# Gate and up projections by token tile, weights in four column chunks, and an activation that is turned through DRAM, in a fused two-layer adaLN/FFN kernel

## Chip, cores and metric

The kernel runs on one core of a Trainium2 chip, as one program. The metric is the device time of one execution in microseconds. Before the change it is 393.52 us, the median of 3 runs (393.29 to 393.7).

## What is computed

Two residual layers over 1024 tokens (32 batches of 32) with 512 channels. Cut to what matters:

```
# layer 0, condition: gated FFN with a LoRA branch whose matrices are picked per batch
gate = x @ W_gate.T + LoRA(x, A_gate[id], B_gate[id]) * 0.5      # 512 -> 1376, rank 16
up   = x @ W_up.T   + LoRA(x, A_up[id],   B_up[id])   * 0.5
act  = silu(gate) * up
y    = act @ W_down.T + LoRA(act, A_down[id], B_down[id]) * 0.5  # 1376 -> 512
# layer 0, ffn: one effective 512x512 matrix from low-rank parts
x = x + y @ W_eff.T + bias
# layer 1: condition with top-2 experts, then RMS norm and an int8-like quantized gated FFN
c = x @ W.T + 2 * sum_e gate_e * (x @ A_e) @ B_e
q, s = quant(rmsnorm(c));  Wgq, Wuq, Wdq = quant rows of Wg, Wu, Wd   # round to -127..127
h = silu(q @ Wgq.T * s * sg) * (q @ Wuq.T * s * su)
x = x + quant(h) @ Wdq.T * s2 * sd
```

## The kernel before

**Precision.** Layer 0 keeps float32 accuracy by splitting each operand into a rounded high part and the rest: ScalarE writes the high half (`copy`, into a `..._hl[HI]` tile), VectorE the low half (`lo`), and TensorE makes three products (`THREE`: high·high, high·low, low·high). So each weight tile costs one ScalarE and one VectorE pass.

**Tiling.** The 1024 tokens are two halves (`n`) of 512. For each half the 1376 hidden channels are 11 tiles of 128 (`FT`), and a step `s` is one of the 22. `gate_up(s)` forms gate and up for 128 channels (output rows) by 512 tokens (output columns): per projection 12 matmuls of 512 columns and, for LoRA, 6 of 256 (two groups of eight batches). `silu` and `make_act` leave the activation with channels on partitions, as `down(s)` wants it: 12 matmuls of 512 columns and 6 of 256, accumulated in four banks over 11 steps. TensorE's order is written out by hand: `gate_up(s+1)`, `down(s)`, and so on. The weights are double-buffered by step (`wg_raw`, `wg_hl`), loaded by SyncE (SP).

**Layer 1's weights** are quantized while the second half runs. For each of 11 tiles `f`: SP loads `nat` (512 KB) and `wdx` (256 KB); VectorE takes maxima (`wq_max`, L1025 and L1028); ScalarE scales (`wq_scale`, L715); VectorE rounds to bf16 (`wq_round`, into `nq`); SP issues three DMA transposes (`turn`, L380 to L382). `nat` and `nq` have two buffers each, and `load_nat(f)` waits for the rounding of tile `f-2`. In the loop of SP `load_nat(f+1)` stands ahead of `turn(f-1)`:

```
for f in range(2, FT):
    wg_1(f + 3)
    wd_1(f + 2)
    load_wdx(f + 1)
    load_nat(f + 1)
    turn(f - 1)
```

All engines and both DMA queues take their instructions strictly in the written order; waits are on semaphores. After the last `down` come `cond` (layer 1's condition), `lora_down(1)`, `z` (W_eff), and the quantized FFN.

Of the kernel before, what the change touches and what calls it, by code (L numbers as in the profile page):

```python
# [4 lines left out]
P = 128  # L12
T = 1024
H = 512
F = 1376
# [34 lines left out]
STEPS = NH * FT  # L50

VU_SLOT = (0, 1, 1, 0)
VU_TURN = (1, 2, 4, 5)
STEP0_TURN = 3
C_FIRST = 17 + 4 * FT
# [6 lines left out]
def build(nc, a, scratch, out):  # L62
# [26 lines left out]
    x_raw = [sb(f"x_raw{n}", [P, KT, NB], fp32) for n in range(NH)]  # L89

    W0 = top[0]
    ad_raw = sb("ad_raw", [P, BATCH, FT * RANK], fp32)
    wg_raw = sb("wg_raw", [P, 2, 2 * H], fp32)
    wg_hl = sb("wg_hl", [P, 2, 2, 2 * H], f32r)
    wd_raw = sb("wd_raw", [P, 2, H], fp32)
    wd_hl = sb("wd_hl", [P, 2, 2, H], f32r)
    b_raw = sb("b_raw", [P, 2, 2, 2 * P], fp32)
    b_hl = sb("b_hl", [P, 2, 2, 2, 2 * P], f32r)
    W1 = top[0]

# [18 lines left out]
    D1 = top[0]  # L119
    consts = sb("consts", [P, CONSTS], fp32)  # L120
# [25 lines left out]
    wdx = sb("wdx", [P, H], fp32)  # L146
    wsd_b = wdx
# [51 lines left out]
    oh_lang = sb("oh_lang", [P, TILES, E8], fp32)  # L199
# [28 lines left out]

    def hf(t):
        return t.bitcast(fp32)  # L230

    with ExitStack() as ctx:
        def sem(name):
            return ctx.enter_context(nc.semaphore(name))
# [71 lines left out]
        def _(sp):  # L306
# [30 lines left out]
            with sp.Fori(0, AGU_SP) as b:  # L337
                load_a("a_gu", agu, b, agu_sp)
# [1404 lines left out]
```

## Time and profile before

| | |
|---|---|
| median of 3 runs | 393.52 us |
| span of the profiled execution | 391.3 us (its own time outside the profiler isn't recorded; the median lies 2.2 us above the span) |
| TensorE busy | 379.0 us, 97% |
| VectorE, ScalarE, GpSimd busy | 252.1, 184.1, 140.7 us |
| DMA | 59.89 MB, mean 153 GB/s |

Busy time is a union over the span, and a busy TensorE means only that matmuls follow one another without a gap. The spacing from one block's start to the next block's start is what a block costs.

### The profile page before, as it was taken

Reading aid. Unit: us, or ns where it says so; the run is one execution under the profiler, and the core shown is the slowest. Engines: PE = TensorE matmul, PEld = TensorE weight load, DVE = VectorE, ACT = ScalarE, POOL = GpSimd, SP = SyncE. Lnnn points to the kernel's source line nnn. Section 1 sums busy time; section 2 is a strip of 40 time slices with the busy share of each in tenths; the row PEclk is TensorE's granted clock in tenths of the full one; section 3 lists DMA queues with packets and bytes.
Section 4 is the critical chain, followed back from the end, with each engine's and each line's share of the span. In section 5 each row is a group of like instructions: output and inputs, shape, how many; then the busy total and the mean of one; then the engine's idle time right before and its main releaser. Section 6 shows DMA issues by size and latency. Waiting matters only on the chain.

```text
span 391.3 us, 5936 instructions
## 1 busy us (share of the span) xinstructions
PE 379.0 (97%) x1997; PEld 301.0 (77%) x1997; DVE 252.1 (64%) x485; ACT 184.1 (47%) x307; POOL 140.7 (36%) x138
## 2 busy tenths in 40 slices
PE   8999999999999999999999999999999999899992
PEld 4688888888888988888888888888889874344441
DVE  5876844444454446656777666755585888999982
ACT  5544733333333334434444444643555635676670
POOL 2877887777401061200112130000000124557751
PEclk9999999999999999999999999999999999999998
DMA  7878443445423232632999987554658422323412
GB/s 293 278 230 304 161 142 142 157 165 162 140 94 107 82 94 97 238 115 86 308 271 239 218 197 181 134 109 147 210 119 179 173 54 54 39 56 85 119 62 80
DMA packets 53126, 59.89 MB, mean 153 GB/s; under 512 B 34658, under 2 KB 37500, under 8 KB 52976
## 3 DMA queue, kind: packets, MB, share of 16 engines
q1 hardware_dynamic: 48055, 48.20, 43.2%
q0 software_dynamic: 4320, 10.49, 8.5%
q10 hardware_dynamic: 728, 0.93, 0.7%
q8 instruction: 11, 0.18, 0.2%
q14 instruction: 12, 0.09, 0.1%
HBM read 50.02 MB, written 2.11 MB: 133 GB/s over the span
## 4 chain that ended last, share of the span: by engine, by line
PE 85%; DVE 5%; DMA 4%; ACT 2%; issue 1%; SPq 1%; DVEq 0%; ACTq 0%
PE ps L1353 31%; PE ps L1402 15%; PE ps L1359 8%; PE ps L1478 6%; PE ps L1524 5%; PE ps L1382 4%; PE ps L1598 4%; PE ps L1628 3%; DMA wg_raw<-w_gu_dram 2%; PE ps L1496 2%; PE ps L1344 2%; PE ps L1414 1%; PE ps L1326 1%; PE ps L1531 1%; DVE hqs L1261 1%
## 5 line engine op out<-in xcount | busy, mean ns | idle before, releaser
L1353 PE MATMUL ps<-x_hl,wg_hl 128*128 128x512 f32 x528 | 128.0, 391 | 0.2 <-ACT wg_hl L574 0.2
L1353 PEld LDWEIGHTS ps<-x_hl,wg_hl 128*128 128x128 f32 x528 | 97.4, 188 | 21.0 <-DVE wg_hl L930 0.9
L496 POOL DMA_INDIRECT b_raw<-b_gu_dram,idx_all x44 | 44.3, 1006 | 93.6 <-DVE b_hl L930 83.3
L1402 PE MATMUL ps<-act_hl,wd_hl 128*128 128x512 f32 x264 | 64.0, 391 | 0.0
L1402 PEld LDWEIGHTS ps<-act_hl,wd_hl 128*128 128x128 f32 x264 | 48.2, 188 | 9.1
L1021 DVE TENSOR_TENSOR act_raw<-ps,sil 128x512 f32<-128x512 f32 x22 | 15.2, 689 | 54.6 <-issue 38.0
L1359 PEld LDWEIGHTS ps<-tg_hl,b_hl 128*128 128x128 f32 x264 | 37.3, 190 | 3.3
L1359 PE MATMUL ps<-tg_hl,b_hl 128*128 128x256 f32 x264 | 38.4, 282 | 0.0
L930 DVE TENSOR_TENSOR wg_hl<-wg_raw,wg_hl 128x1024 fp32r<-128x1024 f32 x22 | 26.9, 1224 | 13.2 <-ACT wg_hl L574 12.4
L538 POOL TENSOR_TENSOR qs<-qs,half 128x1 f32<-128x1 f32 x8 | 4.4, 550 | 85.2 <-DVE qs L1225 85.2
L574 ACT ACTIVATE act_hl<-act_raw 128x512 fp32r<-128x512 f32 x22 | 13.9, 633 | 42.3 <-DVE act_raw L1021 42.3
L547 POOL TENSOR_TENSOR g_sb<-g_sb,u_sb 128x459 f32<-128x459 f32 (+1 forms) x23 | 26.5, 1161 | 19.5 <-ACT g_sb L847 19.3
L715 ACT ACTIVATE nat<-nat,winv 128x512 f32<-128x512 f32 x22 | 14.7, 716 | 38.1 <-DVE winv L1033 38.1
L483 POOL DMA_INDIRECT agu<-a_gu_dram,idx_a x23 | 27.0, 1176 | 12.7 <-issue 6.7
L483 POOL DMA_INDIRECT ad_raw<-a_d_dram,idx_a x24 | 24.2, 1009 | 7.3 <-issue 7.3
L661 ACT ACTIVATE sil<-ps 128x512 f32<-128x512 f32 x22 | 12.9, 586 | 27.2 <-PE ps L1359 27.2
L1524 PE MATMUL ps<-wc_lo_hi,x_hl 128*128 128x512 f32 x96 | 23.6, 395 | 0.0
L1598 PE MATMUL ps<-wq_g,qt 128*128 128x459 bf16 (+1 forms) x96 | 22.6, 357 | 1.0 <-DVE g_sb L1252 1.0
L574 ACT ACTIVATE wg_hl<-wg_raw 128x1024 fp32r<-128x1024 f32 x22 | 23.0, 1045 | 0.2 <-DMA wg_raw<-w_gu_dram 0.2
L1478 PE MATMUL ps<-y_hl,we_hl 128*128 128x512 f32 x96 | 23.0, 394 | 0.0
L1598 PE MATMUL ps<-wq_u,qt 128*128 128x459 bf16 (+1 forms) x96 | 22.6, 358 | 0.0
L930 DVE TENSOR_TENSOR b_hl<-b_raw,b_hl 128x512 fp32r<-128x512 f32 x22 | 15.1, 687 | 10.9 <-ACT b_hl L574 10.9
(171 smaller groups left out, 585.0 us busy)
## 6 DMA issues: line engine op xcount, KB each, us to landing
wg_raw<-w_gu_dram SPq DMA_DIRECT2D x22, 512.0 KB, 4.0
wd_raw<-w_d_dram SPq DMA_DIRECT2D x22, 256.0 KB, 2.8
nat<-w_nat_dram SPq DMA_DIRECT2D x11, 512.0 KB, 4.8
wdx<-w_nat_dram SPq DMA_DIRECT2D x11, 256.0 KB, 2.6
natd<-wd_nat_dram SPq DMA_DIRECT2D x4, 704.0 KB, 5.0
vu_raw<-w_vu_dram SPq DMA_DIRECT2D x3, 512.0 KB, 9.3
out_dram<-r_sb SPq DMA_DIRECT2D x6, 256.0 KB, 2.0
ws_b<-scale_scratch SPq DMA_DIRECT2D x2, 688.0 KB, 5.5
```

What stands on the lines that cost most here:

```text
L483: gp.indirect_dma_start(out=tile[:, b, :], out_offset=None, in_=a[table].rearrange("e p c -> (e p) c"), in_offset=bass.IndirectOffsetOnAxi ...
L496: gp.indirect_dma_start(out=b_raw[:, slot, g, :], out_offset=None, in_=a["b_gu"], in_offset=bass.IndirectOffsetOnAxis(ap=idx_all[:, f, 2 * ...
L547: nc.gpsimd.tensor_tensor(g_sb[:, slot, cols], g_sb[:, slot, cols], u_sb[:, slot, cols], ALU.mult).then_inc(h_made, 1)
L574: return nc.scalar.activation(o, i, ACT.Copy)
L930: return V.tensor_tensor(o, raw, hf(hi), ALU.subtract)
L1353: mm(bank[:], wg_hl[:, slot, w, gu * H + k * P:gu * H + (k + 1) * P], x_hl[n][:, v, k, :], start=(k == 0 and (w, v) == THREE[0]), stop=False)
L1359: last = mm(bank[:, g * GT:(g + 1) * GT], b_hl[:, slot, w, g, gu * P:(gu + 1) * P], tg_hl[:, n, v, gu, g * GT:(g + 1) * GT], start=False, ...
L1382: last = mm(ps[TD][:, g * GT:(g + 1) * GT], ad_hl[:, slot, w, g * P:(g + 1) * P], act_hl[:, slot, v, g * GT:(g + 1) * GT], start=(first an ...
L1402: last = mm(ps[m][:], wd_hl[:, slot, w, m * P:(m + 1) * P], act_hl[:, slot, v, :], start=(first and (w, v) == THREE[0]), stop=False)
L1478: last = mm(ps[m][:], we_hl[:, w, k, m * P:(m + 1) * P], y_of[n][:, v, k, :], start=(k == 0 and (w, v) == THREE[0]), stop=(k == KT - 1 and ...
L1524: mm(ps[CB[t]][:], x_hl[t // 4][:, w, k, (t % 4) * P:(t % 4 + 1) * P], wc_hl[v][:, k, :], start=(k == 0 and (w, v) == THREE[0]), stop=False)
L1598: last = mm(ps[(G_BANK, U_BANK)[gu][c]][:, 0:CH[c]], qt[:, t, k, :], wq(gu, k, slice(CO[c], CO[c] + CH[c])), start=(k == 0), stop=(k == KT ...
```

## The change

Layer 0's gate and up are formed with tokens on output rows. A step `s` (now 32) is 128 tokens by a chunk of 352 channels (320 in the last chunk): `x_hl` is stationary, the weights `wg_hl` stream. Four steps (`t` = 0 to 3) share a chunk `j`, and there are four chunks per half (8 in all). The weights of a chunk (four pieces of 352 KB) have one buffer, raw and split. LoRA: the 64 rank rows of four batches are doubled to 128, high part in one half of the partitions and low part in the other, so 2 matmuls of 352 columns replace 6 of 256. For that the tokens are permuted (`x_p`), so that a 128-token tile holds batches t, t+4, t+8, t+12.

The activation now has tokens on partitions, and `down` (unchanged, 22 of them, named d) wants channels there: VectorE turns 32x32 blocks (`turn_act`), ScalarE's queue writes a chunk to DRAM in four DMAs (`write_act`), and SP reads it back by tiles of 128 channels (`load_act`). So the `down`s of chunk j-1 run during chunk j, and the last three after all gate and up work. x is loaded a second time unpermuted. `wq_round` moves from VectorE to ScalarE.

```
+CW = (352, 352, 352, 320)
+DONE = ((0, 1), (2, 3, 4), (5, 6, 7), (8, 9, 10))     # the downs that chunk c completes
...
+            def next_nat(f):
+                turn(f - 2)
+                load_nat(f)
+                load_wdx(f)
...
+            for i, d in enumerate(downs_of(NCH + 1)):
+                next_nat(2 + i)
+                load_down(d)
...
+            next_nat(9)
+            sp.wait_ge(gate_ready, STEPS)
             sp.dma_start(wc_raw[:], a["wc_t"]).then_inc(wc_in, 16)
...
+            sp.wait_ge(up_ready, STEPS)
+            sp.dma_start(x1_n[1][:], a["x_t"][:, :, NB:T]).then_inc(x_in[2], 16)
+            next_nat(10)
+            for d in downs_of(NCH + 3):
+                load_down(d)
...
+            def write_act(j):
+                n, c = divmod(j, NCH)
+                nb = CW[c] // 32
+                act.wait_ge(turned, NT * (j + 1))
+                for q in range(4):
+                    act.dma_start(act_t[n, CO0[c]:CO0[c] + CW[c], q * P:(q + 1) * P].rearrange("(b i) m -> i b m", i=32),
+                                  act_s[32 * q:32 * q + 32, 0:nb].rearrange("p b t m -> p b (t m)")).then_inc(act_out, 16)
...
+            for s in range(24, STEPS):                 # ScalarE
+                step(s)
+                wq_scale(s - 23)
+                wq_round(s - 23)
...
+            for s in range(24, STEPS):                 # VectorE
+                step(s)
+                wq_max(s - 22)
...
+            def gate_up(s):
+                pe.wait_ge(silu_done, s)
+                base(s, 0)
+                lora(s, 0)
...
+                    pe.wait_ge(act_made, s - 1)
+                base(s, 1)
+                lora(s, 1)
```

What the change moves, where the prediction rests on it. VectorE in the second half, before: one step of the loop, from the product of gate and up (`act_raw`) to the next step's splits of weights and LoRA rows.

```order
L1021 TENSOR_TENSOR act_raw<-ps,sil 128x512 [waits act_lo,wg_used]
L930 TENSOR_TENSOR ad_hl<-ad_raw,ad_hl 128x256
L930 TENSOR_TENSOR wd_hl<-wd_raw,wd_hl 128x512 [waits wd_hi]
L930 TENSOR_TENSOR act_hl<-act_raw,act_hl 128x512 [waits act_hi]
L1025 TENSOR_REDUCE wm<-nat 128x2
L1028 TENSOR_REDUCE wdm<-wdx 128x4
L1039 TENSOR_SCALAR nq<-nat 128x1024 [waits wq_in0]
L930 TENSOR_TENSOR wg_hl<-wg_raw,wg_hl 128x1024 [waits wg_hi]
L930 TENSOR_TENSOR b_hl<-b_raw,b_hl 128x512 [waits b_hi]
```

The same place now, behind step 24; `b_hl` here is the split of step 26's LoRA rows.

```order
L1112 TENSOR_TENSOR act_raw<-ps,sil 128x352 [waits turned,up_ready,silu_done]
L1120 STREAM_TRANSPOSE act_s<-act_raw 128x11x32 [waits act_out,act_made]
L1125 TENSOR_REDUCE wm<-nat 128x2 [waits nat_in0]
L1128 TENSOR_REDUCE wdm<-wdx 128x4 [waits wdx_in]
L1131 TENSOR_SCALAR ws_f<-wm 128x2 [waits wm_step]
L1133 RECIPROCAL winv<-ws_f 128x2 [waits wm_step]
L1015 TENSOR_TENSOR b_hl<-b_raw,b_hl 64x704 [waits b_hi]
```

The maxima (`wm`, `wdm`) of one layer-1 tile stand between two steps as before, but a step is now 128 tokens by 352 channels; the rounding into `nq` has left the engine, and the 32x32 transposes have come. The next split of LoRA rows stands behind the maxima. SP's queue, before, one pass of the loop in the second half:

```order
L374 DMA wdx<-w_nat_dram 128x512 [waits wdx_used]
L368 DMA nat<-w_nat_dram 128x1024 [waits nat_rounded]
L380 DMA_TRANSPOSE wq_g<-nq 128x4x128 [waits nat_rounded]
L381 DMA_TRANSPOSE wq_u_105<-nq 128x2x128
L382 DMA_TRANSPOSE wq_u_106<-nq 128x2x128
L314 DMA wg_raw<-w_gu_dram 128x1024 [waits wg_lo,wg_hi]
L319 DMA wd_raw<-w_d_dram 128x512 [waits wd_lo,wd_hi]
```

SP's queue now, at the end of the second half (its last tile of layer 1, then the loads of down 19):

```order
L452 DMA wc_raw_117<-wc_t_dram 128x2048 [waits gate_ready]
L454 DMA x_again_115<-x_t_dram 128x4x512 [waits up_ready]
L407 DMA_TRANSPOSE wq_g_112<-nq_109 128x4x128 [waits nat_rounded]
L408 DMA_TRANSPOSE wq_u0_74<-nq_109 128x2x128
L409 DMA_TRANSPOSE wq_u1_113<-nq_109 128x2x128
L396 DMA nat_108<-w_nat_dram 128x1024 [waits nat_rounded]
L401 DMA wdx_110<-w_nat_dram 128x512 [waits wdx_used]
L356 DMA wd_raw_58<-w_d_dram 128x512 [waits wd_lo]
L364 DMA a_f_65<-act_scratch 128x512 [waits act_lo,act_out]
```

The load of `nat` moved from ahead of a tile's three transposes to behind them, and `a_f`, which TensorE needs for down 19, stands behind both. TensorE at the same place, before (the logits `h_logits(0)`, then `down(21)` alone, then `cond(0)`):

```order
L1496 MATMUL ps<-awr,x_raw_51 128x136 [waits awr_in,act_made]
L1496 MATMUL ps<-awr,x_raw_51 128x136 x11
L1382 MATMUL ps<-act_hl,ad_hl 128x256 [waits ad_lo,act_lo,wd_lo]
L1382 MATMUL ps<-act_hl,ad_hl 128x256 x5
L1402 MATMUL ps<-act_hl,wd_hl 128x512 x12
L1524 MATMUL ps<-wc_lo_hi,x_hl_49 128x512 [waits x1_lo,silu_done,wc_lo]
```

and now, the second part of down 18, the logits, and the beginning of down 19:

```order
L1512 MATMUL ps<-act_hl,wd_hl 128x512 x12
L1595 MATMUL ps<-awr,x_raw_51 128x136 [waits awr_in,act_made]
L1595 MATMUL ps<-awr,x_raw_51 128x136 x11
L1492 MATMUL ps<-act_hl,ad_hl 128x256 [waits ad_lo,act_lo,wd_lo]
L1492 MATMUL ps<-act_hl,ad_hl 128x256 x5
```

Three `down`s follow the logits where one did.

## Rows read from the trace of the kernel before

**Rows 1.** The page, parts 1 and 2: busy time and granted clock in 40 slices.

```profile
PE 379.0 (97%) x1997; PEld 301.0 (77%) x1997; DVE 252.1 (64%) x485; ACT 184.1 (47%) x307; POOL 140.7 (36%) x138
...
PEclk9999999999999999999999999999999999999998
```

**Rows 2.** Timeline, TensorE, one step (start, us; then duration of the block).

```profile
54.32 0.88 PE L1359 MATMUL ps<-tg_hl,b_hl 128*128 128x256 f32 x6
55.04 2.91 PE L1353 MATMUL ps<-x_hl,wg_hl 128*128 128x512 f32 x12
...
58.50 0.88 PE L1382 MATMUL ps<-act_hl,ad_hl 128*128 128x256 f32 x6
...
61.96 2.88 PE L1353 MATMUL ps<-x_hl,wg_hl 128*128 128x512 f32 x12
```

**Rows 3.** Busy time by stage of the gate/up/down phase.

```profile
core 0: us, PE busy (x) PEld busy (x) DVE busy (x) ACT busy (x) POOL busy (x), PEclk, DMA share, GB/s
120.00:150.00 30.00, 30.00 (x173) 26.34 (x171) 14.11 (x23) 9.62 (x17) 6.25 (x6) 1.00 0.34 110
...
215.00:245.00 30.00, 30.00 (x159) 25.85 (x158) 18.99 (x31) 14.25 (x24) 6.21 (x6) 1.00 0.82 198
```

**Rows 4.** Timeline of the start: first steps of ScalarE and TensorE.

```profile
9.85 1.06 ACT L574 ACTIVATE x_hl<-x_raw 128x1024 fp32r<-128x1024 f32 x1 [0.70 <-DMA x_raw<-x_t_dram]
...
12.92 0.72 ACT L586 ACTIVATE wg_hl<-vu_raw,consts 128x512 fp32r<-128x512 f32 x1 [0.72 <-DMA vu_raw<-w_vu_dram]
...
30.61 2.99 PE L1353 MATMUL ps<-x_hl,wg_hl 128*128 128x512 f32 x12
```

**Rows 5.** Groups by line and form: one instruction's mean in ns behind the comma.

```profile
L574 ACT ACTIVATE wg_hl<-wg_raw 128x1024 fp32r<-128x1024 f32 x22 | 23.0, 1045 | 0.2 <-DMA wg_raw<-w_gu_dram 0.2
...
L574 ACT ACTIVATE b_hl<-b_raw 128x512 fp32r<-128x512 f32 x22 | 13.7, 620 | 14.4 <-DMA b_raw<-b_gu_dram,idx_all 14.4
...
L930 DVE TENSOR_TENSOR wg_hl<-wg_raw,wg_hl 128x1024 fp32r<-128x1024 f32 x22 | 26.9, 1224 | 13.2 <-ACT wg_hl L574 12.4
...
L930 DVE TENSOR_TENSOR b_hl<-b_raw,b_hl 128x512 fp32r<-128x512 f32 x22 | 15.1, 687 | 10.9 <-ACT b_hl L574 10.9
...
L1025 DVE TENSOR_REDUCE wm<-nat 128x2 f32<-128x1024 f32 x5 | 6.1, 1216 | 3.2 <-DMA nat<-w_nat_dram 3.2
...
L1028 DVE TENSOR_REDUCE wdm<-wdx 128x4 f32<-128x512 f32 x5 | 3.4, 677 | 0.0
...
L715 ACT ACTIVATE nat<-nat,winv 128x512 f32<-128x512 f32 x22 | 14.7, 716 | 38.1 <-DVE winv L1033 38.1
...
L959 DVE COPY ag<-agu 128x512 f32<-128x512 f32 x8 | 2.9, 429 | 0.9 <-DMA agu<-a_gu_dram,idx_a 0.9
```

**Rows 6.** Timeline of SP's queue, one pass (start, time that the issue takes).

```profile
215.74 0.33 SPq L368 DMA_DIRECT2D nat<-w_nat_dram  x1
216.11 1.20 SPq L380 DMA_TRANSPOSE wq_g<-nq  x1
...
218.63 1.25 SPq L382 DMA_TRANSPOSE wq_u<-nq  x1
219.98 0.52 SPq L314 DMA_DIRECT2D wg_raw<-w_gu_dram  x1
```

**Rows 7.** DMA issues: count, KB each, median us from issue to landing.

```profile
wd_raw<-w_d_dram SPq DMA_DIRECT2D x22, 256.0 KB, 2.8
nat<-w_nat_dram SPq DMA_DIRECT2D x11, 512.0 KB, 4.8
...
out_dram<-r_sb SPq DMA_DIRECT2D x6, 256.0 KB, 2.0
```

**Rows 8.** Timeline: a DMA issue on ScalarE's queue, and the end of the phase.

```profile
1.16 0.45 ACTq L578 DMA_DIRECT2D vu_raw<-w_vu_dram  x1
...
265.81 2.94 PE L1496 MATMUL ps<-awr,x_raw 128*128 128x136 f32 x24
268.50 0.96 PE L1382 MATMUL ps<-act_hl,ad_hl 128*128 128x256 f32 x6
```

More of the change, by code:

```diff
@@ L795, in _ @@
             h_copy(0)
+            td_split(1)
             act.wait_ge(wst_ready, 1)
@@ new lines, in _ @@
+            step(20)
+            td_mask(0)
+            step(21)
+            b_split(23)
+            y_out(0)
+            make_act(22)
+            turn_act(22)
+            for q in range(KT):
+                x1_add(q)
+            down_split(downs_of(NCH)[1])
+            wq_max(0)
+            b_split(24)
+            w_split(NCH + 2, 0)
+            make_act(23)
+            turn_act(23)
+            w_split(NCH + 2, 1)
+            for q in range(KT):
+                x1_low(q)
+            wq_max(1)
@@ L1378, in down_lora @@
-            def down_lora(s, slot, first, end):
-                pe.wait_ge(ad_lo, s + 1)
-                for g in range(2):
-                    for w, v in THREE:
-                        last = mm(ps[TD][:, g * GT:(g + 1) * GT], ad_hl[:, slot, w, g * P:(g + 1) * P],
-                                  act_hl[:, slot, v, g * GT:(g + 1) * GT], start=(first and g == 0 and (w, v) == THREE[0]),
-                                  stop=(end and g == 1 and (w, v) == THREE[-1]), skip_group_check=True)
-                return last
@@ L1387, in down @@
[L1387 to L1397 removed]
+                        last = mm(ps[TD][:, g * GT:(g + 1) * GT], ad_hl[0:m, slot, w, g * P:(g + 1) * P],
+                                  act_hl[0:m, slot, v, g * GT:(g + 1) * GT], start=(f == 0 and g == 0 and (w, v) == THREE[0]),
+                                  stop=(f == FT - 1 and g == 1 and (w, v) == THREE[-1]), skip_group_check=True)
@@ L1398, in down @@
+                return last
+            def down(d):
+                n, f = divmod(d, FT)
+                slot, rows = d % 2, rows_of(d)
+                pe.wait_ge(wd_lo, d + 1)
+                pe.wait_ge(act_lo, d + 1)
+                if d == 0:
+                    pe.wait_ge(we_lo, KT)
+                if d == FT:
+                    pe.wait_ge(td_masked, 1)
+                if d:
+                    down_lora(d)
                 for m in range(KT):
-                    if first and n:
+                    if d == FT:
@@ L1400, in down @@
                         pe.wait_ge(x1_made, m + 1)
                     for w, v in THREE:
-                        last = mm(ps[m][:], wd_hl[:, slot, w, m * P:(m + 1) * P], act_hl[:, slot, v, :],
-                                  start=(first and (w, v) == THREE[0]), stop=False)
-                if lora_behind:
-                    last = down_lora(s, slot, first, end)
+                        last = mm(ps[m][:], wd_hl[0:rows, slot, w, m * P:(m + 1) * P], act_hl[0:rows, slot, v, :],
+                                  start=(f == 0 and (w, v) == THREE[0]), stop=False)
@@ L1545, in _ @@
             h_logits(0)
-            down(STEPS - 1, 1, 1, end=True)
+            for d in downs_of(CHUNKS - 1):
+                down(d)
             pe.wait_ge(wc_lo, 1)
```

961 lines of the change are left out of this document (506 added, 455 removed).

## Prediction, made before the changed kernel ran

> **What bounds the kernel now.** I read the page first: TensorE is busy 97% of the span and its clock is granted in full in all but the last slice [rows 1], so below about 390 us the kernel gets only by less work on TensorE, and every gap opened there costs its length. Then the windows: through the whole gate/up/down phase TensorE has 30.00 busy us in 30, while VectorE and ScalarE have 14.1 and 9.6 in the first half and 19.0 and 14.3 in the second, and the DMA share goes from 0.34 to 0.82 in the second half, where layer 1's weights are quantized and turned [rows 3]. The reader is to see slack everywhere but on TensorE, and least of it in the second half. Then TensorE's timeline for what a block costs, by starts: six matmuls of 256 columns take 55.04 - 54.32 = 0.72 us (0.120 each), a `down` (six of 256, twelve of 512, equal to a gate or up block) 61.96 - 58.50 = 3.46 us, hence twelve of 512 take 2.74 us (0.228 each) [rows 2].
>
> **The change on TensorE.** Before, 22 steps of two blocks: 22 x 6.92 = 152.2 us. A 352-column matmul is in no row. From 0.120 at 256 and 0.228 at 512 the line gives 0.161, and 0.147 for 320; the bounds, by columns from either row alone, are 0.157 and 0.165. I take the line, since both ends lie on it. Now a step is 28 matmuls (24 base, 4 LoRA): 24 steps x 28 x 0.161 + 8 x 28 x 0.147 = 141.1 us. The gain is **11.1 us** (bounds 8.5 to 13.5), nearly all from LoRA (264 matmuls of 256 become 128). The 22 `down`s are unchanged.
>
> The Trainium skill (TensorE: Matmul & The Clock Gate, section "Wait — 56ns, not 53.3ns?") gives a warm matmul N/2.4 GHz plus about 2.5 ns, 215.7 ns at 512 columns; by that 352 columns cost 149 ns and the gain would be some 22 us. The trace disagrees, with 228 ns for these float32r operands, and I go by the trace.
>
> **Start.** Step 0's work on TensorE shrinks by 6.92 - 28 x 0.161 = 2.4 us, but what ends it isn't its work. The first chunk's weights are 1408 KB instead of 512 KB, ahead of `vu_raw` 2; a 512 KB piece took about 1.3 to 1.8 us there, so it lands 2.3 to 3.1 us later than the 12.92 us of [rows 4], and ScalarE and VectorE split 2816 columns where they split 1024. So I let step 0 end 0.5 us after the 30.61 of [rows 4]: **+2.9 us** (0 to 5).
>
> **First half.** Chunk weights have one buffer, but between the last gate of a chunk and the first of the next stand an up block (2.25) and a `down` (3.46): 5.7 us to cover one silu (0.45), two ScalarE passes and two VectorE passes of 704 columns. Line from [rows 5]: 0.78 and 0.89 us, 0.68 and 0.80 back to back, about 3.2 us in all. The trip through DRAM: four issues on ScalarE's queue at 0.45 [rows 8], 2.0 us to land as a 256 KB store does, 2.8 as a 256 KB load [rows 7], about 7 us against 13 to 20 us before the `down` is due. Both at nothing; uncovered they'd cost 3 and 7 us per chunk. The 32x32 transposes (32, no row) lie between a copy of 512 columns, 0.43, cut to 352, 0.3, and a tensor-tensor of 512, 0.69 [rows 5]; I take 0.45. On an engine half idle they cost nothing.
>
> Against this change speaks the Trainium skill (DMA: Bandwidth & Descriptors, "Anatomy of one DMA"): each DMA has a fixed cost of about 2.0 us, mostly the write receipt, so a trip through DRAM pays it twice. The trace agrees with its 2.0 and 2.8 us [rows 7]. It changes the sum only where the trip isn't covered, which is the tail below.
>
> **Second half, steps 24 to 31.** Here eight steps carry eight tiles of layer 1's weights; before, a tile had 10.4 us of TensorE beside it, now 4.5 (a step) plus 1.25 `down`s on average, 6.5 us. A tile's circle: rounding on ScalarE releases three transposes on SP (219.98 - 216.11 = 3.9 us of queue), **then** the load of `nat` (4.8 to landing) [rows 6, 7], then the maxima on VectorE (1.22 + 0.68 + 0.3, some 2.1), then scaling (2 x 0.72, 1.25 back to back) and rounding (0.95) on ScalarE [rows 5]. Two buffers allow one circle of some 13 us, with the steps between, per two tiles: TensorE's own pace. Nothing is left for lateness, and what waits in it holds back work that TensorE wants: behind VectorE's wait for `nat` stand the LoRA rows of the step after next and the product of the next one. Walked through, with time 0 where TensorE would begin step 24:
> - Step 23's up ends at -3.5. Behind it ScalarE has 1.4 (weights), 1.25, 1.8 (four issues), four x halves 2.1, rounding 0.95: tile 0 is rounded at 4.0, LoRA rows and silu(24) follow at 5.2, where TensorE wants them at 4.5: **0.7**.
> - SP: 4.0 + 3.9 + 4.8 = 12.7 until `nat` 2 is there, maxima 14.8, the LoRA rows of step 26 (0.8) 15.6. TensorE wants them after step 25 and the gate of 26, at 11.6: **4.0**.
> - At the chunk's end ScalarE's four writes wait for VectorE, which waited for tile 4: down 15 is split about **1.1** late, and tile 4 rounded only at 36.5. `nat` 6: 45.2, maxima 47.3, rows of step 30 48.1; TensorE wants them at 44.3: **3.8**.
> - The same two tiles on: `nat` 8 at 58.0, product and transpose of step 31 at 61.0, four writes 62.8, split of down 18 65.0; TensorE wants it at 61.5: **3.5**.
>
> Sum **+13.1 us** (0 if loads land in 2.8 and VectorE isn't caught; 20 if two more steps are).
>
> **Tail.** Count from the end of step 31's up. TensorE has downs 17 and 18 and the logits (2 x 3.46 + 268.50 - 265.81 = 9.6 us) [rows 2, 8] before down 19. Its operand: product and transpose 1.0, writes 2.8, split of down 18 4.3, scaling and rounding of tile 8 6.4, SP's transposes 10.3, issues of `nat`, `wdx`, `wd_raw`, `a_f` 11.8, landing with 1.3 MB in front 15.8, splits 17. **+7.4**. Behind down 19's split each engine turns to tile 10 (`nat` there at about 15), maxima 19.1, scale and round 21.3, split of down 20 23.3; TensorE wants it at 20.5: **+2.8**. Tail **+10.2 us** (6 to 14). In that is room for the clock: it was granted in full in every slice but the last, in which TensorE runs dry [rows 1]; should it fall from 2.4 to 1.2 GHz in a gap, each `down` run so costs 3.46 us more. Queued behind: `cond(0)` and everything later, unchanged.
>
> **Sum** against the profiled span: 391.3 - 11.1 + 2.9 + 13.1 + 10.2 = 406.4 us. The median of the runs lies 2.2 above the span of before, so 408.6; I say **408**.
>
> **Rivals.** A change under 0.2% (0.8 us) can't be told from none here.
> - *Tail alone* (0.18): layer 1's tiles keep up in steps 24 to 31, for 215 to 245 shows a DMA share of 0.82, not 1, and VectorE a third idle [rows 3]. 391.3 - 11.1 + 2.9 + 10.2 = 393.3, median 395.5. Against it: the loop has no slack by its rows.
> - *Faster* (0.12): `a_f` of down 19 arrives in time, because tile 8 is rounded before the writes matter or SP gets past it early. One mechanism, one place: it decides if the way to `a_f` is under 9.6 us instead of 17. With step loop fine too, 391.3 - 11.1 + 2.9 + 2.2 = 385.3. Against: that order is written in three in-order queues.
> - *Same* (0.04): tail alone with a start that loses nothing, 393 to 394.
> - *DMA is the bound* (0.08): the trip adds some 11 MB to a stage whose share is already 0.82 [rows 3]; writes are 512-byte rows. If steps 20 to 31 ran at the DMA's pace, 1.3 x 80 us, 420 to 430.
> - My forecast (0.58): 399 to 420.
>
> **Numbers.** Likeliest 408. Range 394 to 420, which leaves out faster, same and DMA-bound at their far ends, and takes in the tail alone. Faster 0.12, same 0.04, slower 0.84.
>
> **What would show it.** Blocks of 12 base matmuls at 1.93 us and LoRA pairs at 0.32; TensorE without gaps from step 1 to 23; VectorE waiting on the DMA of `nat` before L1125 in steps 24 to 31 and TensorE waiting on VectorE's `b_hl`; a gap of several us ahead of down 19 that ends with `a_f`, and a smaller one ahead of down 20. Wrong if gaps stand in the first half (the trip or the single weight buffer then isn't covered), if a 352-column matmul costs 0.15 or 0.18, or if `nat` lands before VectorE asks.

## Result, and the profile after

The changed kernel takes **420.07 us** (median of 4 executions, 419.39 to 420.86) against 393.45 us (393.29 to 393.7, 4 executions) on the same chip: ratio 1.067, interval 1.065 to 1.0689. It is 26.6 us slower; the profiled span went from 391.3 to 417.6 us. Here and in the experiments, executions over 1.5% above the fastest of their kernel are left out (417.77 us of nat_first, 410.16 of combined).

The page of the changed kernel, parts 1 and 2, against [rows 1]:

```profile
PE 381.7 (91%) x2098; PEld 318.6 (76%) x2101; DVE 279.0 (67%) x537; ACT 210.3 (50%) x349; POOL 110.0 (26%) x110
...
PE   8899998999999999999869787775899999999994
...
PEclk9889999999999999999998999968999999999999
DMA  8995491856845727340787949897055932122622
```

TensorE, busy 97% before, has holes in two places: the first seven slices (10.4 us each) and slices 20 to 29, that is 198 to 303 us, where layer 1's weights are quantized. The clock falls in both. Between them the middle of the kernel is as tight as it was.

Two blocks in the second half, TensorE's timeline (start, duration):

```profile
226.16 2.08 PE L1460 MATMUL ps<-wg_hl,x_hl 128*128 128x352 f32 x12
228.08 0.32 PE L1469 MATMUL ps<-b_hl,tg_hl 128*128 128x352 f32 x1
228.24 0.32 PE L1471 MATMUL ps<-b_hl,tg_hl 128*128 128x352 f32 x1
228.40 2.08 PE L1460 MATMUL ps<-wg_hl,x_hl 128*128 128x352 f32 x12
```

By starts: 12 base matmuls 1.92 us, the LoRA pair 0.32, a matmul of 352 columns 0.160 us; where blocks of 320 follow each other, a step takes 4.08 us, 0.146 per matmul. The waits of TensorE (total us, times, longest):

```profile
PE ps L1492 <- DVE act_hl L1015: 13.0, 4, 5.6
PE ps L1469 <- DVE b_hl L1015: 6.0, 2, 3.4
PE ps L1460 <- DVE wg_hl L1015: 2.1, 2, 1.9
PE ps L1460 <- ACT sil L739: 2.0, 2, 1.2
PE ps L1512 <- DVE wd_hl L1015: 1.6, 1, 1.6
```

**Where the 26 us are.** Two more rows of the kernel before, the first `cond` and the last sum on VectorE (TensorE's and VectorE's timelines):

```profile
272.05 2.88 PE L1524 MATMUL ps<-wc_lo_hi,x_hl 128*128 128x512 f32 x12
...
384.79 0.36 DVE L1313 TENSOR_TENSOR r_own<-o_own,x1t 128x192 f32<-128x192 f32 x1
```

and the same places after, with the start of step 1 ahead:

```profile
35.24 2.17 PE L1460 MATMUL ps<-wg_hl,x_hl 128*128 128x352 f32 x12
...
301.09 2.91 PE L1623 MATMUL ps<-wc_lo_hi,x_hl 128*128 128x512 f32 x12
...
413.35 0.36 DVE L1416 TENSOR_TENSOR r_own<-o_own,x1t 128x192 f32<-128x192 f32 x1
```

Step 1 starts 4.63 us later, `cond(0)` 29.04 us later, the last sum 28.56 us. The last output is there 4.25 us behind that sum instead of 6.51, which gives 2.3 us back: 26.3 in all. It is 4.2 to 4.3 us in the profile of every changed kernel below; no run shows why. To split the 29.04, each block's spacing by starts is compared with its tight value (1.92, 0.16, 0.72, 2.75 and so on); the excess is what it lost, by an idle wait or by running at half clock.

| part | forecast | measured |
|---|---|---|
| gate and up, work on TensorE | -11.1 | 152.2 - 24 x 28 x 0.160 - 8 x 28 x 0.146 = -12.0 |
| start (with the 2.4 us that step 0's own work shrank by) | +2.9 | 4.63 + 2.4 = +7.0 |
| first half | 0 | +3.6 |
| steps 24 to 31, with down 15 | +9.6 | +14.0 |
| hole ahead of down 18 | +3.5 | +5.7 |
| tail, from down 18 on | +10.2 | +10.6 |
| behind `cond(0)` | 0 | -0.5, and -2.3 for the last landing |

### The profile page after: what moved, and what is told of

It reads as the page before. It is cut to its first block, busy times and chain, and to the rows that moved or that the text cites. A ratio compares the mean times of both kernels' runs of the same rounds, so it can differ in the third digit from the quotient of the medians.

```text
span 417.6 us, 5954 instructions
## 1 busy us (share of the span) xinstructions
PE 381.7 (91%) x2098; PEld 318.6 (76%) x2101; DVE 279.0 (67%) x537; ACT 210.3 (50%) x349; POOL 110.0 (26%) x110
## 4 chain that ended last, share of the span: by engine, by line
PE 55%; DVE 15%; DMA 12%; ACT 7%; SPq 6%; issue 3%; ACTq 2%; POOL 0%; DVEq 0%
PE ps L1460 19%; PE ps L1512 9%; PE ps L1535 5%; PE ps L1623 5%; DMA a_f<-act_scratch 5%; PE ps L1492 2%; DMA wg_raw<-w_gu_dram 2%; DVE hqs L1364 2%; DVE g_sb L1355 2%; DVE u_sb L1358 2%; ACT nat L768 2%; ACTq L691 2%; PE ps L1698 2%; PE ps L1446 2%; DMA act_scratch<-act_s 2%
## 5 line engine op out<-in xcount | busy, mean ns | idle before, releaser
L1460 PE MATMUL ps<-wg_hl,x_hl 128*128 128x352 f32 (+1 forms) x768 | 135.6, 326 | 5.6 <-DVE wg_hl L1015 2.1
L1460 PEld LDWEIGHTS ps<-wg_hl,x_hl 128*128 128x128 f32 x768 | 125.7, 193 | 11.2 <-issue 5.3
L1512 PE MATMUL ps<-act_hl,wd_hl 128*128 128x512 f32 (+1 forms) x264 | 66.9, 404 | 1.6 <-DVE wd_hl L1015 1.6
L1512 PEld LDWEIGHTS ps<-act_hl,wd_hl 128*128 128x128 f32 (+1 forms) x264 | 50.4, 197 | 11.7 <-DVE wd_hl L1015 1.9
L739 ACT ACTIVATE sil<-ps 128x352 f32<-128x352 f32 (+1 forms) x32 | 14.6, 457 | 56.4 <-PE ps L1471 55.2
L1015 DVE TENSOR_TENSOR wg_hl<-wg_raw,wg_hl 128x704 fp32r<-128x704 f32 (+1 forms) x32 | 26.3, 863 | 13.0 <-ACT wg_hl L624 13.0
L1492 PE MATMUL ps<-act_hl,ad_hl 128*128 128x256 f32 (+1 forms) x132 | 21.0, 298 | 13.0 <-DVE act_hl L1015 13.0
L624 ACT ACTIVATE b_hl<-b_raw 64x704 fp32r<-64x704 f32 (+1 forms) x32 | 24.8, 774 | 14.2 <-PE ps L1471 7.4
L1015 DVE TENSOR_TENSOR b_hl<-b_raw,b_hl 64x704 fp32r<-64x704 f32 (+1 forms) x32 | 27.8, 870 | 5.8 <-ACT b_hl L624 4.8
L1469 PE MATMUL ps<-b_hl,tg_hl 128*128 128x352 f32 (+1 forms) x64 | 20.9, 326 | 6.3 <-DVE b_hl L1015 6.0
L624 ACT ACTIVATE wg_hl<-wg_raw 128x704 fp32r<-128x704 f32 (+1 forms) x32 | 23.1, 770 | 4.9 <-PE ps L1471 2.9
L1120 DVE STREAM_TRANSPOSE act_s<-act_raw 128x352 f32<-128x352 f32 (+1 forms) x32 | 17.2, 537 | 11.1 <-DMA act_scratch<-act_s 10.1
```

The lines of the kernel that those rows point to most:

```text
L624: return nc.scalar.activation(o, i, ACT.Copy)
L1015: return V.tensor_tensor(o, raw, hf(hi), ALU.subtract)
L1120: V.transpose(act_s[:, 0:nb, t, :], act_raw[:, 0:CW[c]]).then_inc(turned, 1)
L1460: mm(bank[:, 0:w], x_hl[n][:, v, k, t * P:(t + 1) * P], wg_hl[gu][:, u, k, 0:w], start=(k == 0 and (v, u) == THREE[0]), stop=False)
L1469: mm(bank[:, 0:w], tg_hl[:, HI, gu, t * P:(t + 1) * P], b_hl[:, s % 2, gu * w:(gu + 1) * w], start=False, stop=False)
L1492: last = mm(ps[TD][:, g * GT:(g + 1) * GT], ad_hl[0:m, slot, w, g * P:(g + 1) * P], act_hl[0:m, slot, v, g * GT:(g + 1) * GT], start=(f == ...
```

## Why layer 1's tiles hold up the gates

SP's queue, changed kernel, around the first hole of the second half:

```profile
207.12 1.31 SPq L407 DMA_TRANSPOSE wq_g<-nq  x1
208.48 1.23 SPq L408 DMA_TRANSPOSE wq_u<-nq  x1
209.75 1.25 SPq L409 DMA_TRANSPOSE wq_u<-nq  x1
211.04 0.59 SPq L396 DMA_DIRECT2D nat<-w_nat_dram  x1
```

VectorE:

```profile
210.57 0.55 DVE L1120 STREAM_TRANSPOSE act_s<-act_raw 128x352 f32<-128x352 f32 x1
215.42 1.22 DVE L1125 TENSOR_REDUCE wm<-nat 128x2 f32<-128x1024 f32 x1 [4.30 <-DMA nat<-w_nat_dram]
...
217.54 0.89 DVE L1015 TENSOR_TENSOR b_hl<-b_raw,b_hl 64x704 fp32r<-64x704 f32 x1
```

and TensorE:

```profile
218.48 0.56 PE L1469 MATMUL ps<-b_hl,tg_hl 128*128 128x352 f32 x1 [3.44 <-DVE b_hl L1015]
...
219.13 3.42 PE L1460 MATMUL ps<-wg_hl,x_hl 128*128 128x352 f32 x12
```

Read them downwards. Rounding of tile 0 (ended 207.1) releases three transposes, 3.9 us of issuing; only then goes the load of `nat` 2, which lands 4.4 us later. VectorE stands 4.30 us at `wm`; behind it waits the split of step 26's LoRA rows, and TensorE stands 3.44 us for that. The block behind the hole then takes 3.25 us by starts (219.13 to 222.38) where it should take 1.92. The same wait stands three more times for 3 to 5 us (until 231.6, 251.6 and 265.9); the first held the split of chunk 7's weights (hole of 1.93 us ahead of step 28), the second step 30's rows (2.51), the third step 31's product and with it down 18 (5.57).

## The experiments

Each kernel was timed beside the kernel before on its chip; those of one group below ran on the same chip. A ratio is not exactly the quotient of the two medians. For size: 0.01 is 3.9 us.

| kernel | median us | ratio to before, interval |
|---|---|---|
| changed | 420.07 | 1.067, 1.065 to 1.0689 |
| nat_first | 411.3 | 1.0443, 1.0423 to 1.0464 |
| loads_first | 408.26 | 1.0398, 1.036 to 1.0436 |
| tail_loads | 423.31 | 1.0771, 1.0741 to 1.0801 |
| fill_holes | 419.58 | 1.0675, 1.0623 to 1.0728 |
| third_first | 409.73 | 1.043, 1.0392 to 1.0469 |
| tail_order | 406.22 | 1.0315, 1.0247 to 1.0383 |
| no_trip | 416.83 | 1.0622, 1.0553 to 1.069 |
| gate_whole | 417.31 | 1.0625, 1.0599 to 1.0651 |
| combined | 403.54 | 1.03, 1.0218 to 1.0382 |
| combined_hold | 406.6 | 1.0329, 1.0312 to 1.0346 |
| combined_late | 400.07 | 1.0143, 1.0109 to 1.0178 |
| combined_light | 403.0 | 1.0245, 1.0206 to 1.0285 |

### First group: the order of SP's queue, and the clock

**nat_first**

```
 def next_nat(f):
-    turn(f - 2)
     load_nat(f)
     load_wdx(f)
+    turn(f - 2)
```

> SP issues the loads of nat and wdx of tile f ahead of the three transposes of tile f-2, as before the change; nothing else moves. Theory A (order in SP's queue): nat of tiles 2, 6 and 8 comes 3.9 us earlier, so the 3.44 us gap ahead of step 26's LoRA rows and the 2.51 us gap at step 30 go, and with them the half-clock stretch behind the first (1.3 us); the gap ahead of down 18 loses up to 3 us. Together 7 to 12 us, 408 to 413. Theory B (pace: DMA is full in these steps and a tile's circle is too long in any order): the transposes only come later in turn, gaps move, and the time stays within 2 us of 420.

8.8 us faster, theory A. The order alone, which the change had turned round, was worth a third of the loss: from the start of step 24 to that of down 18 TensorE takes 56.9 us instead of 65.6.

**loads_first**: the load of the next down's operands goes ahead of the transposes too (`load_nat`, `load_wdx`, `load_down(d)`, `turn(f - 2)`).

> As the run before, and the loads of wd_raw and a_f of the next down also stand ahead of the transposes. Theory A: the down operands land 4 us earlier too, which helps where ScalarE waited for a_f (4.8 to 5.5 us each, and queued behind that wait are the scaling and rounding of the next tile): another 2 to 4 us, 405 to 410. Theory B: no more than the run before, within 2 us of 420.

11.8 us faster than the changed kernel, 3.0 of them beyond the run before (their intervals overlap, so this part is not shown). From step 24 to down 18 it takes 53.7 us. The same place of TensorE's timeline, loads_first:

```profile
210.90 2.08 PE L1460 MATMUL ps<-wg_hl,x_hl 128*128 128x352 f32 x12
213.12 0.43 PE L1469 MATMUL ps<-b_hl,tg_hl 128*128 128x352 f32 x1
```

2.22 us from start to start: the hole of 3.44 is down to some 0.3, and the clock is whole behind it. In 200 to 260 us the busy time of TensorE rose from 49.20 to 53.52 us (first row changed kernel, second loads_first; the columns behind PEclk are DMA share and GB/s):

```profile
200.00:260.00 60.00, 49.20 (x278) 45.04 (x277) 40.37 (x71) 36.07 (x58) 4.18 (x4) 0.97 0.81 220
```

```profile
200.00:260.00 60.00, 53.52 (x318) 49.43 (x316) 45.97 (x83) 40.06 (x66) 4.17 (x4) 1.00 1.01 263
```

So the DMA engines, with a share of 0.81, were not the limit in the changed kernel's loop; the same work packed tighter makes it 1.01. Whether they are the limit at 1.01 is another question, which combined_light takes up.

**tail_loads**

```
+for d in downs_of(NCH + 3)[0:2]:
+    load_down(d)
 next_nat(10)
-for d in downs_of(NCH + 3):
-    load_down(d)
+load_down(downs_of(NCH + 3)[2])
```

> Only in the tail: the loads for downs 19 and 20 stand ahead of the transposes of tile 8 and the loads of tile 10. Theory A: a_f of down 19 is issued at about 275.5 instead of 280.9, lands some 4 us earlier behind wc and x, so the 4.22 us gap and the slow clock behind it (1.5 us) go, but nat 10 comes later and the gap ahead of down 20 may grow: net 3 to 6 us, 414 to 417. Theory B (the 2 MB of wc and x in front of it set the landing): 0 to 1.5 us, 418.5 to 420.

Wrong on both sides: 3.2 us slower. SP's queue, tail_loads:

```profile
268.56 0.94 SPq L356 DMA_DIRECT2D wd_raw<-w_d_dram  x1
278.79 0.33 SPq L364 DMA_DIRECT2D a_f<-act_scratch  x1
...
280.11 1.22 SPq L407 DMA_TRANSPOSE wq_g<-nq  x1
```

SP stood 9.3 us at `a_f` until the last chunk's writes had landed, with tile 8's transposes and `nat` 10 behind it, so the hole ahead of down 20 grew from 1.63 to 4.81 us while down 19's stayed at 4.02. Ahead of the transposes `a_f` was issued 2.2 us earlier than in the changed kernel (278.79 against 280.95) and not 5: what held it there was the writes.

**fill_holes**: matmuls with an all-zero stationary operand in the holes (22 of them ahead of down 18, for instance), so that TensorE doesn't idle.

```
+for _ in range(count):
+    mm(bank[:, 0:w], zeros[:], x_hl[1][:, HI, 0, 0:w], start=False, stop=False)
 pe.wait_ge(b_lo, s + 1)
```

> TensorE gets matmuls with an all-zero operand in the holes (5 of 512 columns bf16 in the start, 18 of 352 ahead of step 26's LoRA rows, 22, 16 and 6 of 512 ahead of downs 18, 19 and 20); no operand comes earlier. Theory A (a hole costs its length and then the clock: 2.4 to 1.2 GHz behind the holes at 15, 215, 269 and 284 us): the granted clock stays at 1.00 and 7 to 10 us come back, 410 to 413. Theory B (only the holes' lengths count, or the clock falls for another reason, such as the DMA load): within 1 us of 420, or slower by what the added matmuls overrun.

Theory A's mechanism is there and its price is not. Busy time, granted clock, DMA share and GB/s in the tail, changed kernel:

```profile
274.00:280.00 6.00, 6.00 (x17) 0.50 1.08 371
```

and fill_holes, with the start of its down 19:

```profile
274.00:280.00 6.00, 6.00 (x44) 1.00 1.16 315
...
287.37 1.50 PE L1498 MATMUL ps<-act_hl,ad_hl 128*128 128x256 f32 x6 [3.40 <-DVE wd_hl L1019]
```

Down 18 ran at 2.4 instead of 1.2 GHz, it and the logits behind it ended 3 us earlier, and down 19 still began at 287.4 us, where it had begun at 287.47. Its operand was on its way through DRAM and knows nothing of the clock; what the clock gave back, the next hole took. Ahead of step 28 the same happened: its hole grew from 1.93 to 3.18 us. In a stretch bound by another chain, half clock costs nothing, and a list of excess times counts that loss twice over.

### Second group: the trip, the tail and the start

**third_first** (on loads_first), ScalarE at the end of a chunk:

```
-write_act(j)
 if j and len(downs_of(j - 1)) == 3:
     down_split(downs_of(j - 1)[2])
+write_act(j)
```

> The run with all loads ahead of the transposes (408.3), and on ScalarE the split of a chunk's third down now stands ahead of the four writes of the next chunk's activation. Theory A (down 18 waits for the writes' place in ScalarE's queue, its own operand having landed long before): its split starts some 3.4 us earlier, the 3.97 us gap ahead of down 18 and the half clock behind it (1.1 us) go, but the four writes start 1.5 us later and so does a_f of down 19, whose gap (6.67 us) takes the rest: net 0 to 3 us, 405 to 408. Theory B (down 18 waits for its operand): no change, or slower by the later writes.

The hole ahead of down 18 fell from 3.97 to 0.86 us, so it was the place in ScalarE's queue; but the one ahead of down 19 grew from 6.67 to 12.61 us in the profiled executions. In time it is no different from loads_first (intervals overlap), and outside the 405 to 408 of theory A.

**tail_order** (on third_first): SP issues wc, `turn(7)`, `load_down(19)`, `load_down(20)`, `nat` and `wdx` of tile 10, `turn(8)`, x, `load_down(21)`; both split engines take wc behind down 19 and tile 10 behind down 20.

> The run before, and the tail rewritten in three queues: SP issues wc, the transposes of tile 7, then the loads of downs 19 and 20, then nat and wdx of tile 10 and the transposes of tile 8, and x again only behind them; ScalarE and VectorE split down 19 ahead of wc and down 20 ahead of tile 10. Theory A (the gap of 6.67 us ahead of down 19 is the writes landing late behind 2 MB of other loads, and the queue's order): with 1 MB taken out of the way the writes land in 5 us instead of 9, the gap falls to 2 to 4 us and the one ahead of down 20 stays under 1: 400 to 404. Theory B (the trip through DRAM has this length in any order): 405 to 408.

406.22, in theory B's range, with executions from 403.56 to 408.85. The hole ahead of down 19 is 6.29 us, hardly smaller than loads_first's 6.67, with 1 MB fewer in front, and one of 3.94 us stands ahead of down 21. SP's queue, tail_order; ScalarE issued the four writes from 255.96 to 258.2 us:

```profile
260.84 0.60 SPq L356 DMA_DIRECT2D wd_raw<-w_d_dram  x1
265.87 0.33 SPq L364 DMA_DIRECT2D a_f<-act_scratch  x1
```

The writes were counted 7.7 us behind the last issue: theory A's "5 instead of 9" didn't come. The DMA share from 256 to 266 us was still 0.97, so this run didn't show the writes on free engines.

**no_trip** (on tail_loads): `a_f` is read from the table of down weights, with no wait for the writes, so downs multiply other numbers; SP waits for the writes only behind down 21's loads.

> The run tail_loads (423.3), and a_f is read from the down weights' table in DRAM instead of the written activation, with no wait for the writes; the activation is still written, so only the output's meaning is lost. It prices the round trip's latency. Theory A (in tail_loads SP stood still until the writes of the last chunk landed, 9 us after issue, with the transposes of tile 8 and nat 10 behind it): that gap goes, and SP runs on: 412 to 416. Theory B (the trip is covered and the loop's pace sets the time): 422 to 424. Should steps 24 to 31 gain as well, the trip isn't covered there either.

5.9 us faster by the ratios (1.0771 to 1.0622), nearest to theory A, a little short of its 412 to 416. SP issued `a_f` of down 19 at 269.32 instead of 278.79 us, and the hole ahead of down 19 fell from 4.02 to 1.28 us (down 20: 4.81 to 4.06). Steps 24 to 31 gained nothing: the hole ahead of step 26's LoRA rows was 3.57 us (3.53 in tail_loads), and from step 24 to down 18 TensorE took 64.9 us (63.7). So in the loop the trip is covered, and the wait for `nat` is the cause there; in the tail the trip is the cause of the hole ahead of down 19.

**gate_whole**, TensorE in the start:

```
 base(0, 0, terms=THREE[0:1])
+base(0, 0, terms=THREE[1:])
 base(0, 1, terms=THREE[0:1])
 pe.wait_ge(urs_ready, 1)
 mm(ps[TD][0:4, :], smalls[0:4, s_at["r"]], ur[:], ...)
-base(0, 0, terms=THREE[1:])
```

> The changed kernel (420.07), and in the start all three terms of step 0's gate stand ahead of its up: 8 matmuls that have their operands fill the hole in which TensorE waited 1.2 us for the up weights. Theory A (the hole takes the clock from 2.4 to 1.2 GHz for the next 6.5 us): the granted clock stays at 1.00, the 16 matmuls behind take 0.16 each instead of 0.30, and step 1 starts 2.5 to 4 us earlier, 416 to 417.5. Theory B (the start ends with the gather of the LoRA matrices and vu 3, whatever TensorE does before): step 1 starts within 0.5 us of where it did, 419.5 to 420.5.

1.8 us faster by the ratios (the intervals touch), 2.8 by the medians. TensorE, busy time, clock, DMA share and GB/s in the start, changed kernel:

```profile
18.00:24.00 6.00, 6.00 (x19) 0.50 1.04 344
```

and gate_whole, with its step 1:

```profile
18.00:24.00 6.00, 4.62 (x26) 1.00 1.02 359
...
31.81 2.18 PE L1460 MATMUL ps<-wg_hl,x_hl 128*128 128x352 f32 x12
```

In the changed kernel TensorE was idle from 14.68 to 15.90 us, waiting for the up weights, and from about 17.2 to 24 us its clock was 0.50, 1.2 GHz. With eight ready matmuls in the hole it stays at 2.4 GHz, and step 1 starts at 31.81 instead of 35.24 us. One execution of each overstates this. Over the profiles of all kernels, step 1 starts between 33.28 and 35.24 us without this edit (8 kernels, mean clock in 6 to 32 us 0.87 or 0.93, fill_holes' 0.93 among them) and between 31.81 and 32.75 with it (5 kernels, 1.00 in four and 0.93 in one). So it brings some 2 us, and the clock, 0.07 to 0.13 of 26 us, is of that size. Here nothing later swallows it. The edit also puts work into the hole of 1.2 us, so what the hole was worth and what the clock was worth are not told apart. The Trainium skill (TensorE: Matmul & The Clock Gate, section "What's actually happening") has the same two levels and takes idleness as what lowers the clock; that agrees with these rows, except that holes of 1.14 and 1.38 us in gate_whole's own start lowered nothing.

### Third group: together, and what is left

**combined**: loads_first, third_first, tail_order and gate_whole.

> Four edits together: all loads ahead of the transposes (measured -11.8), the third down's split ahead of the writes (+1.5), the tail's order (-3.5 on top), step 0's gate whole ahead of its up (-2.8). If what the start gains isn't lost again in the loop behind it (theory: 125 us without a gap lie between), the sum holds: 420.1 - 11.8 + 1.5 - 3.5 - 2.8 = 403.5, with 401 to 406. Rival: the engines' queues in steps 24 to 31 take the start's gain back, 406 to 408.

403.54 by the median (402.91, 403.54 and 408.37), as forecast, and 405.5 by the ratio: with so wide an interval not told apart from tail_order. Steps 25 to 31 are nearly tight: in 200 to 260 us TensorE is busy 57.26 us of 60. Holes of 6.23 us ahead of down 19 and 2.91 ahead of down 21 are left.

**combined_hold**, TensorE: `down(16)` behind `gate_up(31)` instead of ahead of it.

> The combined kernel, and on TensorE down 16 stands behind step 31 instead of between steps 30 and 31. Theory A (the hole ahead of down 19 is a trip of fixed length, product to split about 16 us, against 9.6 us of cover in downs 17, 18 and the logits): 3.5 us more of cover take up to 3.5 us from the gap, if step 31 really is formed earlier: 1 to 3.5 us faster than combined. Theory B (step 31's product waits for VectorE, which waits for nat of tile 8, so that nothing starts earlier): the gap appears ahead of step 31 instead, within 1 us of combined.

No gain (1.0329 against 1.03). Down 19 began at 267.97 us against 268.62, and a new hole of 1.39 us stood ahead of step 31: theory B.

**combined_light**: downs 13 to 21 load 16 of 128 rows of their weights.

```
-sp.dma_start(wd_raw[:, d % 2, :], a["w_d"][d % FT])
+m = 16 if d >= 13 else P
+sp.dma_start(wd_raw[0:m, d % 2, :], a["w_d"][d % FT][0:m])
```

> The combined kernel, and for downs 13 to 21 only 16 of the 128 rows of the down weights are loaded (the others keep old values, so the output loses its meaning; same number of DMAs, 2 MB less of the 21 MB moved between 200 and 300 us). Theory A (the DMA engines are full in steps 24 to 31 and in the tail, their share 1.0, and what lands late lands late for bandwidth): 2 to 5 us faster than combined. Theory B (latencies and the order of queues, not bytes): within 1 us of combined.

No different as a time (1.0245 against 1.03, intervals overlap, spans 401.4 and 401.7), theory B. Two windows, combined:

```profile
230.00:260.00 30.00, 28.92 (x175) 26.49 (x174) 23.29 (x45) 20.78 (x33) 0.00 (x0) 1.00 1.03 276
256.00:262.00 6.00, 6.00 (x40) 5.51 (x41) 3.41 (x6) 4.57 (x6) 0.00 (x0) 1.00 1.04 365
```

and combined_light, where everything here comes 2 us earlier, with the landing times of its last writes and loads of the activation:

```profile
230.00:260.00 30.00, 29.14 (x181) 26.86 (x181) 22.43 (x42) 21.75 (x34) 0.00 (x0) 1.00 0.87 245
254.00:260.00 6.00, 6.00 (x41) 5.51 (x41) 3.40 (x6) 4.57 (x6) 0.00 (x0) 1.00 1.06 333
...
DMA to landing us min/median/max: 2.8/6.4/8.2
```

In 230 to 260 us the DMA share fell from 1.03 to 0.87 and TensorE gained 0.2 us: with the queues in this order, bytes are not what is left in the loop. The trip of the last chunk is not settled by this run. While its writes were under way (second rows) the share was 1.06 against 1.04, since `nat` and the 1 MB of wc were issued around them as before; the bytes saved lie ahead of and behind that (0.61 against 0.81 in 260 to 290 us). The writes took up to 8.2 us and the hole ahead of down 19 was 6.46 us (6.23 in combined). That full DMA engines make the writes slow stays untested.

**combined_late** (on combined): tile 10 behind downs 20 and 21 in all three queues, and `silu(s)` ahead of `b_split(s + 1)` in a chunk's first step.

> The combined kernel, with two more moves. Tile 10 of layer 1 (nat, maxima, scaling, rounding) goes behind the splits and loads of downs 20 and 21 on SP, VectorE and ScalarE; and on ScalarE the silu of a chunk's first step goes ahead of the split of the next LoRA rows. The 3.94 us gap ahead of down 21 (its a_f was issued behind nat 10, the transposes and the 1 MB of x) should go with the half clock there (1.4 us), and some 1 us each at steps 4 and 24: 5 to 8 us faster than combined. Against it: the transpose of the scales on TensorE waits for tile 10's maxima, which may open a gap of 1 to 4 us behind cond(0).

1.57 points of the ratio less than combined, some 6 us, as forecast, and clear of its interval; by the medians it is 3.5 us, so the size is loose. TensorE, combined_late, from the logits on:

```profile
261.31 2.94 PE L1603 MATMUL ps<-awr,x_raw 128*128 128x136 f32 x24
271.41 1.62 PE L1500 MATMUL ps<-act_hl,ad_hl 128*128 128x256 f32 x6 [7.15 <-DVE act_hl L1023]
...
276.40 0.87 PE L1500 MATMUL ps<-act_hl,ad_hl 128*128 128x256 f32 x6
...
279.85 0.88 PE L1500 MATMUL ps<-act_hl,ad_hl 96*128 96x256 f32 x6
```

Downs 20 and 21 follow without a hole, and the scales' transpose opened none. One large hole, of 7.15 us, is left, the trip's, and some of 1.4 to 1.8 us ahead of step 6's LoRA rows, down 0 and down 18. This is the best version made, still 1.4% slower than the kernel before.

## The prediction, step by step

**The number.** 408 was forecast and 420.07 measured, just at the upper end of the range (420): 14.6 us of loss were forecast, 26.6 came. The kind of loss was right, its size was not. What is missing lies in the start (4.1 us), the first half (3.6) and steps 24 to 31 with the hole ahead of down 18 (6.6).

**What bounds the kernel.** Right: each gap on TensorE cost its length, up to the point that fill_holes shows, where a later wait swallows it.

**The change on TensorE, -11.1.** Right, measured -12.0; a 352-column matmul takes 0.160 us, the line's 0.161. The formula of the Trainium skill that the prediction names (TensorE: Matmul & The Clock Gate, section "Wait — 56ns, not 53.3ns?") gives 149 ns, and the trace disagrees here too. The prediction's "some 22 us" sets this formula after the change against the trace before it. With the formula on both sides the gain is 142.7 - 130.7 = 12.0 us (an estimate from its figures), so it would hardly have moved the sum. The bounds, too, redone from 0.157 and 0.165 us, are 7.7 to 14.9 us, not 8.5 to 13.5.

**Start, +2.9: mis-sized, measured +7.0.** The bytes were counted and the holes between the pieces not. The DMA share in 6 to 32 us is 1.01, against 0.80 before, which fits pieces that come late; no run takes bytes away here. The up weights arrived 1.2 us too late for TensorE, and behind that hole the clock fell: 16 matmuls took 0.30 us each (18.81 to 23.67 us) instead of 0.16, 2.3 us. [rows 1] had shown whole clock in the start of the kernel before, and from that I priced a fall only in the tail.

**First half, nothing: wrong, +3.6.** The step that failed is "the trip ... about 7 us against 13 to 20". ScalarE and SP, changed kernel, first chunk:

```profile
50.64 2.77 ACTq L691 DMA_DIRECT2D act_scratch<-act_s  x4
...
63.62 0.63 ACT L624 ACTIVATE wd_hl<-wd_raw 128x512 fp32r<-128x512 f32 x1 [5.48 <-DMA a_f<-act_scratch]
```

```profile
59.04 0.81 SPq L364 DMA_DIRECT2D a_f<-act_scratch  x2
```

13 us from the first issue to the split, and down 0 stood 1.64 us for it. Part 6 of the page has the sizes (KB, median us to landing):

```profile
a_f<-act_scratch SPq DMA_DIRECT2D x20, 256.0 KB, 4.5
act_scratch<-act_s ACTq DMA_DIRECT2D x24, 176.0 KB, 5.0
```

5.0 and 4.5 us, where [rows 7] gave 2.0 for a store at the quiet end of the kernel and 2.8 for a load. I took the price of a DMA from a stage with free engines. Beside these writes ran the 1 MB of x (9.4 us to landing); whether that slowed them was not tested. The 2.0 us that the prediction takes from the Trainium skill (DMA: Bandwidth & Descriptors, "Anatomy of one DMA") stand there for DMAs issued from GpSimd, not from SP and ScalarE, and for the part that doesn't grow with the bytes. In the rest of the first half TensorE lost nothing to the trip. What remains of the 3.6 us is silu 4 behind the four issues (0.85) and small waits.

The writes have a second waiter, which the prediction left out: `act_s` has one buffer, so VectorE's first transpose of the next chunk waits until the chunk before has landed.

```profile
59.12 0.55 DVE L1120 STREAM_TRANSPOSE act_s<-act_raw 128x352 f32<-128x352 f32 x1 [3.35 <-DMA act_scratch<-act_s]
```

Here this cost TensorE nothing. In nat_first the wait was 6.39 us and TensorE stood 2.20 us for the LoRA rows of step 6, split behind it. In no_trip, where the read waits for nothing, it was 5.58 us; down 0 had no hole then, the rows of step 6 had one of 1.39, and from step 1 to step 24 nothing was gained (173.0 us; changed kernel 173.2).

**Steps 24 to 31: right in mechanism, 14.0 instead of 9.6.** Silu 24: 1.3 (forecast 0.7). Step 26: 3.6 (4.0). Down 15: 1.7 (1.1). Step 30: 2.7 (3.8). Not seen: the hole of 1.93 us ahead of step 28, where the same wait for `nat` held the split of chunk 7's weights, and the half clock behind the first hole (1.3). nat_first shows the cause, and no_trip that the trip isn't it. That `nat` landed in 4.0 us (median), less than the 4.8 assumed, didn't help. There is a slip in the forecast pace: five `down`s stand beside the eight steps, 0.6 per step and not 1.25; 4.5 + 0.6 x 3.46 gives the 6.5 us that the prediction went on with.

**Down 18, +3.5: measured 5.7.** As described, its split stood behind ScalarE's writes, which waited for VectorE; third_first shows the place in the queue. But `nat` 8 again held the product first.

**Tail, +10.2: measured 10.6, with wrong parts; that the sums agree is luck.** Forecast 7.4 ahead of down 19 and 2.8 ahead of down 20; the waits were 4.22 and 1.63, and nearly all the rest is half clock, 2.9 in down 18 and 1.4 in down 19, for which I had kept "room". The reason given was half right. I put `a_f` behind the transposes and `nat` 10 in SP's queue and let the writes land in 2 us; the last four took 9.0 (median), and tail_loads shows that ahead of the transposes SP would have waited nearly as long. fill_holes shows that the half clock there is no separate cost.

**Rivals.** *DMA is the bound*: by its price (420 to 430) nearest to the measured time, by its mechanism not borne out; the share was 0.81 in 200 to 260 us, and the same bytes in another order took 11.8 us less. Its 11 MB are those of the whole kernel; half of them move in the second half. It stays open only for the start (share 1.01) and for the last chunk's writes. *Tail alone* and *faster* failed on the loop and on the trip's length.

## What to carry to other kernels

Where a change makes steps shorter, walk each in-order queue at the new pace: work that was harmless beside 10 us of matmuls, a tile's load behind three transposes, here stopped three engines beside 6.5. A round trip through DRAM is priced from DMAs of a stage as busy as the one it will run in, and is worth it only while the next chunk's work covers it; the last chunk has only two `down`s and the logits for cover. Count who waits for the written buffer to come free, too, and not only who reads. Before counting a clock loss or a hole as a gain to be had, ask whether the next operand would be there any earlier.

## What was not expected of the hardware

In the changed kernel's start a hole of 1.2 us on TensorE was followed by nearly 7 us at half clock, while in its second half holes of 1.93, 1.57 and 2.51 us were followed by whole clock, and those of 3.44 us and more by half. Over the other kernels the length doesn't sort them: half clock came behind 2.00 us in no_trip (0.50 from 240 to 242 us) and behind 2.20 in combined_light (0.50 from 280 us), and whole clock behind 3.32 in fill_holes (1.00 from 254 to 258 us). In the start the size of the fall also changes between kernels with the same order of work (mean in 6 to 32 us 0.87 to 0.93). What decides it was not found.

A DMA store from SBUF to DRAM had 2.0 us to landing for 256 KB at the end of the kernel before, and 9.0 us for 160 KB in the changed tail. The Trainium skill (DMA: Bandwidth & Descriptors, section "Issuing engines are not separate DMA queues") says that transfers of all issuing engines interleave on the same 16 engines. The share of 1.03 from 269 to 280 us, while these writes were under way, fits that, and combined_light's 1.06 at the same place with writes of up to 8.2 us does too; no run has these writes on free engines. The writes' 512-byte rows, or the transposes and 1 MB loads issued just ahead of them, may be the cause as well; no run separates these, and it stays open.

The kernel before took 392.49 to 394.22 us in all 21 executions beside the experiments. Kernels with holes scattered by up to 5.8 us (no_trip 414.98 to 420.73, tail_order 403.56 to 408.85): once the time hangs on when DMAs land, it varies as they do, and edits worth under 2 us can't be told apart in a few executions.
